# A fused LoRA feed-forward kernel: normalising the down projection's rows straight from PSUM

## The chip, the cores and the metric

One core of a Trainium2 chip runs the whole program. The metric is the device time of one execution in microseconds (us), taken as the median of several runs. The engines are named as in the profile: PE is TensorE's matrix multiply and PEld its weight load, DVE is VectorE, ACT is ScalarE, POOL is GpSimd, SP is the engine that issues most of the transfers.

## The reference

There are 4096 tokens: 128 entries of 32 tokens, 512 features each. Every entry has one of 16 LoRA adapters (rank 16, scale 0.5).

```python
def lora_add(base, inp, A, B):
    t = einsum('bri,bni->bnr', A[idx], inp)
    return base + einsum('bor,bnr->bno', B[idx], t) * 0.5
gate = lora_add(x @ W_gate.T, x, A_gate, B_gate)      # 512 -> 1376
up   = lora_add(x @ W_up.T,   x, A_up,   B_up)
act  = silu(gate) * up
down = lora_add(act @ W_down.T, act, A_down, B_down)  # 1376 -> 512
amax = clip(max(abs(down), axis=-1), 1e-5)            # per token
out  = ((down / amax) @ Wq.T) * (amax * weight_scale) + bias
result = x + out
```

`Wq` holds the four levels -1.5, -0.5, 0.5, 1.5.

## The kernel before, in words

The tokens, sorted by adapter, are worked through in 16 tiles of 256, each of two sub-tiles of 128 rows (`SUBS`, index `s`). The 1376 hidden features are cut into 11 chunks (`FC`, index `f`), the first 96 wide, the others 128. Every operand of a product is split into a high and a low part, and three matrix products (`PASSES`) stand for one.

Each engine has an instruction order of its own, written by hand, and semaphores tie the orders together. Tile 0 is coded apart, since it also brings in the weights; tiles 1 to 15 run in a loop. On the data of this profile no tile has more than two adapters, and the branch with `pair` true runs.

The feed-forward stage of a tile is not done at its end but inside the next tile's first chunks. In tile `t` PE does, in this order: chunk 0 of gate and up (`first_chunk_main`); the last chunk of the down projection of tile t-1 (`last_down`); chunk 1 of gate and a third of chunk 1 of up; the two LoRA products of chunk 0 (L1142); `lora_b_down(t-1)` (L1218), which completes `ps_down` for tile t-1 and counts up `blocks_done`; the rest of up 1 and the two LoRA products of chunk 1 (L1145); gate 2 with its LoRA product (L1145), up 2; the LoRA product of act chunk 0 (`lora_a_down`, L1189); and `down(t, 0)` (L1207), the first to write `ps_down` again. `ps_down` has one buffer, two PSUM banks, so `down(t, 0)` has to wait until the old contents have been taken out. After `down(t, 1)` PE transposes the normalised rows (`transpose_block`, L1229), and in later chunks multiplies them with `wq` (`ffn_block`).

Before, ACT copies both sub-tiles of `ps_down` to `norm` in SBUF (`drain_down`, L635, semaphore `drained`), and `down(t, 0)` waits for these two copies. `norm` is a part of the tensor `rows`, and the profile shows it under that name. DVE then finds each row's largest magnitude in `norm` (`block_scales`: a reduction over 512 columns at L854, a clip at L857, a reciprocal at L860 that counts up `rinv_ready`, a product at L861), and ACT scales `norm` in place (`normalise`, L639, semaphore `norm_ready`).

In the chunk loop ACT's order is `silu_gate(f)` (L696; L688 for chunk 0), `split_hi_b(f+2)` (L628), then the copies when f is 0, `split_hi_act(f)` (L707), then `normalise` when f is 1 or 2. DVE's order is `gate_times_up(f)` (L943; for chunk 0 `add_first_lora`, which ends with L937 and counts up `act_done`), `split_lo_b(f+2)` (L829), `split_lo_act(f)` (L949), `split_ad(f+1)` (L843, L845), then `block_scales(f)` when f is 0 or 1. POOL's `split_bd` (L561, L566) splits the LoRA rows of down as soon as `blocks_done` allows it. The last tile has no next one: there `block_scales` and `normalise` read `ps_down` already, and the diff leaves that part alone.

Of the kernel before, what the change touches and what calls it, by code (L numbers as in the profile page):

```python
# [35 lines left out]
ACT = mybir.ActivationFunctionType  # L36
# [50 lines left out]
def build(nc, x_tok, x_feat, lora_index, places, pair_masks, w_gu, w_down, w_2bit, a_gu, a_down, b_rows,  # L87
          scale_col, bias_rows,
          block_mask_in, identity_in, out):
    with ExitStack() as ctx:  # L90
# [138 lines left out]
        act_hi = sem("act_hi")  # L229
        act_lo = sem("act_lo")  # L230
        amax_steps = sem("amax_steps")
        drained = sem("drained")
        rinv_ready = sem("rinv_ready")
        norm_ready = sem("norm_ready")
        dt_hi = sem("dt_hi")
# [372 lines left out]
        def _(act):  # L608
# [20 lines left out]
                                     b_raw[0:n, at:at + 2 * w].rearrange("p (g w) -> p g w", g=2), ACT.Copy  # L629
                                     ).then_inc(b_hi, 1)  # L630

            def drain_down(tile, s):

                act.wait_ge(blocks_done, SUBS * tile + s + 1)
                nc.scalar.activation(norm[:, s, :], ps_down[:, s, :], ACT.Copy).then_inc(drained, 1)  # L635

            def normalise(tile, s, source):
                act.wait_ge(rinv_ready, SUBS * tile + s + 1)
                nc.scalar.activation(norm[:, s, :], source[:, s, :], ACT.Copy, scale=rinv[:, s:s + 1]  # L639
# [70 lines left out]
            def run_tile(tile, first, pair):  # L710

                if first:
                    if pair:
                        act.wait_ge(first_a_in, 32)
                    else:
                        act.wait_ge(a_in, a_loads(0, pair))
                    for k in range(KC):
                        nc.scalar.activation(a_split_chunk(0, k, loras(pair)), a_raw_chunk(k, loras(pair)),
                                             ACT.Copy).then_inc(a_hi, 1)
                act.wait_ge(x_in, 16 * ENTRIES * (tile + 1))  # L720
                if not first:
                    act.wait_ge(up_done, FC * tile)
                nc.scalar.activation(xs_split(0), x_by_chunk, ACT.Copy).then_inc(x_hi, 1)
                if first:
                    load_wgu(act, 2)
                    load_wd(act, 0)
                    load_wd(act, 1)
                    split_hi_wgu(2)
                    split_hi_t(tile, pair)
                    split_hi_b(tile, 0, pair)  # L730
                    split_hi_b(tile, 1, pair)
                    if pair:
                        copy_first_gate(tile, first)
                        copy_first_up(tile, first)
                    split_hi_wd(0)
                else:
                    split_hi_act(tile - 1, FC - 1, False)
                    split_hi_b(tile, 0, pair)
                    split_hi_b(tile, 1, pair)
                    if pair:  # L740
                        copy_first_gate(tile, first)
                        copy_down_lora(tile - 1)
                    split_hi_t(tile, pair)
                    if pair:
                        split_hi_down_lora(tile - 1)
                        copy_first_up(tile, first)
                for f in range(FC):
                    if first and 1 < f < FC - 1:
                        split_hi_wd(f + 1)
                    if first and 1 < f < FC - 2:  # L750
                        split_hi_wgu(f + 2)
                    silu_gate(tile, f, first, pair)
                    if first and f == 1:
                        split_hi_wgu(3)
                    if f < FC - 2:
                        split_hi_b(tile, f + 2, pair)
                    if not first and f == 0:
                        for s in range(SUBS):
                            drain_down(tile - 1, s)
                    if f < FC - 1:  # L760
                        split_hi_act(tile, f, first)
                    if first and f <= 1:
                        split_hi_wd(f + 1)
                    if not first and f in (1, 2):
                        normalise(tile - 1, f - 1, norm)
                    if not first and f in (2, 4):
                        split_hi_transposed(tile - 1, f // 2 - 1, ps_misc[:, :])

# [35 lines left out]
        def _(dve):  # L804
# [42 lines left out]
            def block_scales(tile, s, source):  # L847

                done = 2 * (SUBS * tile + s)
                if source is ps_down:  # L850
                    dve.wait_ge(blocks_done, SUBS * tile + s + 1)
                else:
                    dve.wait_ge(drained, SUBS * tile + s + 1)
                nc.vector.tensor_reduce(amax[:, s:s + 1], source[:, s, :], AX_X, ALU.max,  # L854
                                        apply_absolute_value=True).then_inc(amax_steps, 1)
                dve.wait_ge(amax_steps, done + 1)
                nc.vector.tensor_scalar(amax[:, s:s + 1], amax[:, s:s + 1], EPS, None, ALU.max  # L857
                                        ).then_inc(amax_steps, 1)
                dve.wait_ge(amax_steps, done + 2)
                nc.vector.reciprocal(rinv[:, s:s + 1], amax[:, s:s + 1]).then_inc(rinv_ready, 1)  # L860
                nc.vector.tensor_tensor(ascale[:, s:s + 1], amax[:, s:s + 1], wscale[:, :], ALU.mult  # L861
                                        ).then_inc(ffn_scaled, 1)
# [89 lines left out]
            def run_tile(tile, first, pair):  # L952

                if first:
                    for k in range(KC):
                        dve.wait_ge(a_hi, k + 1)
                        last = nc.vector.tensor_tensor(a_split_chunk(1, k, loras(pair)),
                                                       a_raw_chunk(k, loras(pair)),
                                                       a_split_chunk(0, k, loras(pair)).bitcast(F32), ALU.subtract)
                    last.then_inc(a_ready, 1)  # L960
                dve.wait_ge(x_hi, tile + 1)
                nc.vector.tensor_tensor(xs_split(1), x_by_chunk, xs_split(0).bitcast(F32), ALU.subtract
                                        ).then_inc(x_lo, 1)
                if first:
                    if not pair:
                        dve.wait_ge(mask_ready, 2)
                    mask_t(tile, pair)
                    split_lo_t(tile, pair)
                    split_lo_b(tile, 0, pair)
                    split_lo_wgu(2)  # L970
                    split_lo_b(tile, 1, pair)
                    split_lo_wd(0)
                else:
                    split_lo_act(tile - 1, FC - 1)
                    split_lo_b(tile, 0, pair)
                    split_lo_b(tile, 1, pair)
                    mask_t(tile, pair)
                    mask_down_lora(tile - 1, pair)
                    split_lo_t(tile, pair)
                    split_lo_down_lora(tile - 1, pair)  # L980
                split_ad(tile, 0, pair)
                for f in range(FC):
                    if first and 1 < f < FC - 1:
                        split_lo_wd(f + 1)
                        if f + 1 >= WQ_FROM:
                            convert_wq(f + 1 - WQ_FROM)
                    if first and 1 < f < FC - 2:
                        split_lo_wgu(f + 2)
                    if pair and f == 0:
                        add_first_lora(tile)  # L990
                    else:
                        gate_times_up(tile, f)
                    if first and f == 1:
                        split_lo_wgu(3)
                    if f < FC - 2:
                        split_lo_b(tile, f + 2, pair)
                    if f < FC - 1:
                        split_lo_act(tile, f)
                        split_ad(tile, f + 1, pair)
                    if first and f <= 1:  # L1000
                        split_lo_wd(f + 1)
                    if not first and f in (0, 1):
                        block_scales(tile - 1, f, norm)
                    if not first and f in (2, 4):
                        split_lo_transposed(tile - 1, f // 2 - 1, ps_misc[:, :])
                    if not first and f in (3, 5):
                        scale_and_bias(tile - 1, f // 2 - 1, ps_misc[:, :])
                if first:

                    dve.wait_ge(const_in, 48 if pair else 32)  # L1010
# [77 lines left out]
        def _(pe):  # L1088
# [110 lines left out]
            def down(tile, f, first):  # L1199
                w = WIDTHS[f]  # L1200
                if first:
                    pe.wait_ge(wd_lo, f + 1)
                elif f == 0:
                    pe.wait_ge(drained, SUBS * tile)
                for s in range(SUBS):
                    for n, (ap, wp) in enumerate(PASSES):
                        last = nc.tensor.matmul(ps_down[:, s, :], act_split[0:w, ap, f % 2, s * P:(s + 1) * P],  # L1207
# [162 lines left out]
```

## Time and profile before

| | |
|---|---|
| median of 3 runs | 966.0 us (965.61 to 966.6) |
| span of the profiled execution | 963.2 us |
| PE busy | 926.2 us, 96% of the span |
| DVE busy | 473.5 us, 49% |
| ACT busy | 337.6 us, 35% |
| POOL busy | 117.3 us, 12% |
| granted TensorE clock, mean | 0.994 |

The span runs from the first to the last instruction of the profiled execution. What lies around it, as far as the runs tell, is the difference to their median, 2.8 us. Times in the rows are us from the start of the span, durations are us unless the view says ns, and an instruction's start can lie a little ahead of the end of the one before it on the same engine, because engines are pipelined.

### The profile page before, as it was taken

What the parts mean: (1) busy time and instruction counts of PE and PEld (TensorE: products, weight loads), DVE (VectorE), ACT (ScalarE), POOL (GpSimd) and SP (SyncE); (2) the same over time, 40 slices, a digit from 0 to 9 for tenths busy, and PEclk for the clock granted to TensorE, in tenths of its full rate; (3) what the DMA queues carried; (4) which work ended last, traced back from release to release, by engine and by line L of the source; (5) the groups of instructions that cost most, each with busy time, mean ns of one, the idle gap of its engine ahead of it and who ended that gap; (6) DMA issues with size and microseconds to landing.
All of it is one profiled execution on the core that took longest, in us unless ns stands there. A gap on an engine that the chain in (4) does not pass through costs nothing.

```text
span 963.2 us, 21495 instructions
## 1 busy us (share of the span) xinstructions
PE 926.2 (96%) x6426; PEld 860.0 (89%) x6426; DVE 473.5 (49%) x1268; ACT 337.6 (35%) x778; POOL 117.3 (12%) x188
## 2 busy tenths in 40 slices
PE   4799999999999999999999999999999999999994
PEld 4799998999999999999999999999999999999993
DVE  3776345363543636345363643536354363634533
ACT  2545233242423425243242423325243242423421
POOL 0110200111010110200111020110200111020100
PEclk9999999999999999999999999999999999999998
DMA  4672212121121112212111121212212111221010
GB/s 135 196 203 58 63 40 58 36 54 44 47 61 37 53 34 58 58 42 58 36 53 43 50 61 37 58 26 61 55 44 58 36 52 42 52 61 36 23 33 25
DMA packets 56679, 54.83 MB, mean 57 GB/s; under 512 B 20080, under 2 KB 41968, under 8 KB 56656
## 3 DMA queue, kind: packets, MB, share of 16 engines
q1 hardware_dynamic: 55056, 52.08, 20.7%
q10 hardware_dynamic: 1600, 2.49, 0.8%
q8 instruction: 8, 0.13, 0.1%
q14 instruction: 15, 0.12, 0.0%
HBM read 46.14 MB, written 8.39 MB: 57 GB/s over the span
## 4 chain that ended last, share of the span: by engine, by line
PE 86%; DVE 5%; issue 3%; DMA 2%; SPq 2%; ACT 1%; DVEq 0%; ACTq 0%
PE ps_down L1207 24%; PE ps_up L1110 23%; PE ps_gate L1110 22%; PE ps_misc L1238 6%; PE ps_td L1189 4%; DVE b_split L829 2%; PE ps_gate L1145 2%; PE ps_up L1145 2%; PE ps_misc L1229 1%; DMA rows<-w_2bit 1%; DVE act_full L932 1%; ACT act_full L688 1%; DVE wgu L807 1%; DMA ad_raw<-pair_masks 1%; DMA rows<-w_down 0%
## 5 line engine op out<-in xcount | busy, mean ns | idle before, releaser
L1207 PE MATMUL ps_down<-wd,act_split 128*128 128x512 f32 (+1 forms) x1056 | 272.9, 394 | 0.0
L1110 PE MATMUL ps_up<-xs,wgu 128*128 128x256 f32 x1920 | 259.7, 284 | 0.0
L1110 PE MATMUL ps_gate<-xs,wgu 128*128 128x256 f32 x1920 | 258.4, 285 | 0.0
L1110 PEld LDWEIGHTS ps_gate<-xs,wgu 128*128 128x128 f32 x1920 | 248.8, 191 | 9.1
L1110 PEld LDWEIGHTS ps_up<-xs,wgu 128*128 128x128 f32 x1920 | 244.7, 192 | 1.3
L943 DVE TENSOR_TENSOR act_full<-ps_up,act_full 128x256 f32<-128x256 f32 x160 | 67.7, 423 | 309.7 <-PE ps_up L1145 309.7
L1207 PEld LDWEIGHTS ps_down<-wd,act_split 128*128 128x128 f32 (+1 forms) x1056 | 185.9, 188 | 31.1
L696 ACT ACTIVATE act_full<-ps_gate 128x256 f32<-128x256 f32 x160 | 60.5, 378 | 283.4 <-PE ps_gate L1145 283.4
L628 ACT ACTIVATE b_split<-b_raw 64x256 fp32r<-64x256 f32 (+1 forms) x176 | 70.2, 407 | 115.2 <-PE ps_up L1145 115.2
L707 ACT ACTIVATE act_split<-act_full 128x256 fp32r<-128x256 f32 (+1 forms) x176 | 73.1, 415 | 88.9 <-DVE act_full L943 84.1
L829 DVE TENSOR_TENSOR b_split<-b_raw,b_split 32x256 fp32r<-32x256 f32 (+1 forms) x176 | 86.9, 500 | 5.3 <-ACT b_split L628 0.4
L575 POOL TENSOR_TENSOR rows<-rows 128x512 f32<-128x512 f32 x30 | 38.7, 1289 | 358.0 <-DVE rows L924 358.0
L949 DVE TENSOR_TENSOR act_split<-act_full,act_split 128x256 fp32r<-128x256 f32 (+1 forms) x176 | 74.9, 425 | 13.2 <-ACT act_split L707 8.2
L1189 PE MATMUL ps_td<-act_split,ad_split 128*32 128x256 f32 (+1 forms) x352 | 69.5, 279 | 3.1 <-DVE act_split L949 3.1
L561 POOL TENSOR_TENSOR bd_split<-bd_raw,ones 64x512 fp32r<-64x512 f32 x16 | 16.9, 1057 | 430.2 <-PE ps_down L1218 388.9
L1238 PE MATMUL ps_misc<-wq,dt_split 128*128 128x512 f32 x248 | 62.7, 396 | 0.6 <-DVE dt_split L866 0.6
L1238 PEld LDWEIGHTS ps_misc<-wq,dt_split 128*128 128x128 f32 x248 | 47.6, 192 | 10.9 <-issue 0.9
L1145 PE MATMUL ps_gate<-t_split,b_split 96*128 96x256 f32 x160 | 47.2, 295 | 5.1 <-DVE b_split L829 5.1
L924 DVE SCALAR_TENSOR_TENSOR rows<-ps_misc,ascale,bias 128x512 f32<-128x512 f32 x31 | 23.3, 751 | 56.6 <-PE ps_misc L1238 56.6
L1189 PEld LDWEIGHTS ps_td<-act_split,ad_split 128*32 128x32 f32 (+1 forms) x352 | 43.0, 124 | 6.1 <-issue 4.3
L1145 PE MATMUL ps_up<-t_split,b_split 96*128 96x256 f32 x160 | 45.2, 282 | 0.0
L1145 PEld LDWEIGHTS ps_gate<-t_split,b_split 96*128 96x128 f32 x160 | 30.8, 192 | 8.2 <-DVE b_split L829 8.1
(90 smaller groups left out, 684.1 us busy)
## 6 DMA issues: line engine op xcount, KB each, us to landing
rows<-x_tok SPq DMA_DIRECT2D x128, 64.0 KB, 1.7
x_raw<-x_feat SPq DMA_DIRECT2D x124, 64.0 KB, 1.7
out<-rows SPq DMA_DIRECT2D x124, 64.0 KB, 1.6
b_raw<-b_rows SPq DMA_DIRECT2D x64, 92.0 KB, 2.9
b_raw<-b_rows SPq DMA_DIRECT2D x64, 80.0 KB, 2.5
rows<-w_gu SPq DMA_DIRECT2D x8, 512.0 KB, 4.1
rows<-w_down SPq DMA_DIRECT2D x9, 256.0 KB, 4.2
bd_raw<-b_rows SPq DMA_DIRECT2D x64, 32.0 KB, 1.7
```

The costliest lines, as they stand in the source:

```text
L575: pool.tensor_tensor(out_rows[:, s, :], x_res[:, s, :], out_rows[:, s, :], ALU.add).then_inc(out_ready, 1)
L628: nc.scalar.activation(b_split[0:n, 0, f % 2, :, 0:w], b_raw[0:n, at:at + 2 * w].rearrange("p (g w) -> p g w", g=2), ACT.Copy).then_inc(b_ ...
L696: nc.scalar.activation(act_full[0:w, f % 2, :], ps_gate[0:w, f % 2, 0:TILE], ACT.Silu).then_inc(silu_done, 1)
L707: nc.scalar.activation(act_split[0:w, 0, f % 2, :], act_full[0:w, f % 2, :], ACT.Copy).then_inc(act_hi, 1)
L829: nc.vector.tensor_tensor(lo, b_raw[0:n, at:at + 2 * w].rearrange("p (g w) -> p g w", g=2), b_split[0:n, 0, f % 2, :, 0:w].bitcast(F32), A ...
L943: nc.vector.tensor_tensor(act_full[0:w, f % 2, :], ps_up[0:w, f % 2, 0:TILE], act_full[0:w, f % 2, :], ALU.mult).then_inc(act_done, 1)
L949: nc.vector.tensor_tensor(act_split[0:w, 1, f % 2, :], act_full[0:w, f % 2, :], act_split[0:w, 0, f % 2, :].bitcast(F32), ALU.subtract).th ...
L1110: last = nc.tensor.matmul(ps_out[0:m, f % 2, 0:TILE], w, xs[:, xp, k, :], start=(start and k == 0), stop=(stop and k == KC - 1))
L1145: last = nc.tensor.matmul(ps_out[0:w, f % 2, 0:TILE], b_split[0:STACK, 0, f % 2, g, 0:w], t_split[0:STACK, 0, g, :], start=False, stop=True)
L1189: last = nc.tensor.matmul(ps_td[0:m, 0:TILE], ad_split[0:w, f % 2, 0:m], act_split[0:w, part, f % 2, :], start=(f == 0 and part == HI), st ...
L1207: last = nc.tensor.matmul(ps_down[:, s, :], act_split[0:w, ap, f % 2, s * P:(s + 1) * P], wd[0:w, wp, f, :], start=(f == 0 and n == 0), st ...
L1238: last = nc.tensor.matmul(ps_block, dt[:, part, k, :], wq[:, k, :], start=(part == HI and k == 0), stop=(part == LO and k == KC - 1))
```

## The change

The two copies of `ps_down` go. `block_scales` and `normalise` of tile t-1 read `ps_down` itself, as they did already in the last tile. `block_scales(0)` and `block_scales(1)` move up on DVE, to just behind the product of gate and up of chunks 0 and 1. `normalise(0)` and `normalise(1)` move up on ACT by one chunk, to the end of chunks 0 and 1. The next tile's first write to `ps_down` waits for `norm_ready`, for both sub-tiles, in place of `drained`.

```diff
-            def drain_down(tile, s):
-
-                act.wait_ge(blocks_done, SUBS * tile + s + 1)
-                nc.scalar.activation(norm[:, s, :], ps_down[:, s, :], ACT.Copy).then_inc(drained, 1)
...
-                    if not first and f == 0:
-                        for s in range(SUBS):
-                            drain_down(tile - 1, s)
                     if f < FC - 1:
                         split_hi_act(tile, f, first)
                     if first and f <= 1:
                         split_hi_wd(f + 1)
-                    if not first and f in (1, 2):
-                        normalise(tile - 1, f - 1, norm)
+                    if not first and f in (0, 1):
+                        normalise(tile - 1, f, ps_down)
...
             def block_scales(tile, s, source):
-                if source is ps_down:
-                    dve.wait_ge(blocks_done, SUBS * tile + s + 1)
-                else:
-                    dve.wait_ge(drained, SUBS * tile + s + 1)
+                dve.wait_ge(blocks_done, SUBS * tile + s + 1)
...
                         gate_times_up(tile, f)
                     if first and f == 1:
                         split_lo_wgu(3)
+                    if not first and f in (0, 1):
+                        block_scales(tile - 1, f, ps_down)
                     if f < FC - 2:
                         split_lo_b(tile, f + 2, pair)
...
-                    if not first and f in (0, 1):
-                        block_scales(tile - 1, f, norm)
...
                 elif f == 0:
-                    pe.wait_ge(drained, SUBS * tile)
+                    pe.wait_ge(norm_ready, SUBS * tile)
```

## Rows read from the trace of the kernel before

**Rows 1.** Busy time by engine over one steady tile: us, busy (instructions), clock, DMA

```profile
200.00:257.58 57.58, 57.23 (x402) 53.32 (x401) 27.90 (x77) 20.04 (x47) 7.46 (x12) 1.00 0.19 48
```

**Rows 2.** Waits of PE from 84 to 940 us: total us, times, longest

```profile
PE ps_gate L1145 <- DVE b_split L829: 5.1, 15, 0.3
```

**Rows 3.** Timeline around one change of tile: start, duration, engine, line

```profile
257.83 1.03 POOL L561 TENSOR_TENSOR bd_split<-bd_raw,ones 64x512 fp32r<-64x512 f32 x1 [26.17 <-PE ps_down L1218]
...
258.20 0.94 DVE L937 TENSOR_TENSOR act_full<-ad_raw,act_full 96x256 f32<-96x256 f32 x1 [0.16 <-ACT act_full L688]
...
258.38 1.05 ACT L635 ACTIVATE rows<-ps_down 128x512 f32<-128x512 f32 x2
...
258.94 1.36 POOL L566 TENSOR_TENSOR bd_split<-bd_raw,bd_split 32x512 fp32r<-32x512 f32 x1
259.17 1.41 DVE L829 TENSOR_TENSOR b_split<-b_raw,b_split 32x256 fp32r<-32x256 f32 x1
...
259.64 0.37 ACT L696 ACTIVATE act_full<-ps_gate 128x256 f32<-128x256 f32 x1
...
260.61 0.42 DVE L949 TENSOR_TENSOR act_split<-act_full,act_split 96x256 fp32r<-96x256 f32 x1
...
260.63 0.39 PE L1145 MATMUL ps_gate<-t_split,b_split 96*128 96x256 f32 x1 [0.34 <-DVE b_split L829]
...
261.27 0.68 DVE L854 TENSOR_REDUCE amax<-rows 128x1 f32<-128x512 f32 x1
...
262.31 0.42 DVE L943 TENSOR_TENSOR act_full<-ps_up,act_full 128x256 f32<-128x256 f32 x1
262.40 1.25 PEld L1207 LDWEIGHTS ps_down<-wd,act_split 96*128 96x128 f32 x6
...
262.76 0.42 DVE L829 TENSOR_TENSOR b_split<-b_raw,b_split 32x256 fp32r<-32x256 f32 x1
...
263.08 0.71 ACT L639 ACTIVATE rows<-rows,rinv 128x512 f32<-128x512 f32 x1
...
263.70 0.36 ACT L696 ACTIVATE act_full<-ps_gate 128x256 f32<-128x256 f32 x1
...
263.92 0.26 PEld L1189 LDWEIGHTS ps_td<-act_split,ad_split 128*32 128x32 f32 x2
```

**Rows 4.** Timeline of the last tile's end, where the source is PSUM already

```profile
945.65 0.69 DVE L854 TENSOR_REDUCE amax<-ps_down 128x1 f32<-128x512 f32 x1
...
946.56 0.16 DVE L860 RECIPROCAL rinv<-amax 128x1 f32<-128x1 f32 x1
...
946.76 0.69 ACT L639 ACTIVATE rows<-ps_down,rinv 128x512 f32<-128x512 f32 x1 [0.36 <-DVE rinv L860]
...
947.50 0.42 PEld L1229 LDWEIGHTS ps_gate<-ad_raw,rows 128*128 128x128 f32 x4 [0.63 <-ACT rows L639]
```

**Rows 5.** Timeline of POOL and DVE in tile 0

```profile
43.70 2.16 POOL L566 TENSOR_TENSOR bd_split<-bd_raw,bd_split 32x512 fp32r<-32x512 f32 x1
...
44.63 0.41 DVE L943 TENSOR_TENSOR act_full<-ps_up,act_full 128x256 f32<-128x256 f32 x1
45.07 1.07 DVE L829 TENSOR_TENSOR b_split<-b_raw,b_split 32x256 fp32r<-32x256 f32 x1
```

**Rows 6.** One DVE line: ns shortest/median/longest, first and last start

```profile
L820 DVE TENSOR_SCALAR wq<-rows x4: 427/427/540, 58.0 to 73.0; 128x512 fp32r<-128x512 int32 x4
```

**Rows 7.** Timeline of PE in tile 0, its two longest waits there

```profile
26.46 0.46 PE L1142 MATMUL ps_misc<-t_split,b_split 96*96 96x256 f32 x2 [3.02 <-DVE b_split L829]
...
41.27 0.39 PE L1189 MATMUL ps_td<-act_split,ad_split 128*32 128x256 f32 x2 [1.48 <-DVE act_split L949]
```

**Rows 8.** Windows of tile 0: columns as in rows 1

```profile
24.00:28.00 4.00, 1.54 (x8) 1.57 (x9) 2.89 (x5) 2.98 (x7) 0.00 (x0) 0.85 0.40 123
28.00:32.00 4.00, 4.00 (x26) 3.92 (x26) 3.65 (x12) 2.28 (x6) 0.00 (x0) 0.73 0.35 111
...
41.40:45.00 3.60, 3.60 (x26) 3.34 (x26) 2.74 (x4) 2.13 (x4) 2.73 (x2) 1.00 0.74 244
```

More of the change, by code:

```diff
@@ L231, in build @@
         amax_steps = sem("amax_steps")
-        drained = sem("drained")
         rinv_ready = sem("rinv_ready")
```

## The prediction, made before the changed kernel was run

> **What bounds the kernel now.** I read three views in this order. The windows come first, with a window as long as one steady tile: PE is busy 57.23 of 57.58 us at the full clock of 2.4 GHz (granted share 1.00), and DVE and ACT are busy for half of that or less [rows 1]. The reader is to see that a steady tile has 0.35 us in which PE does nothing. The table of waits names it: from tile 1 to near the end PE waits for one thing only, DVE's split of the LoRA rows of chunk 2, 15 times 0.34 us [rows 2, 3]. So PE's order sets the time, and an edit can gain at most 5.1 us in the steady tiles, while every wait that it adds to PE costs its full length, 15 times over (the wait in the diff stands in tiles 1 to 15). The timeline around one change of tile is then the working sheet. I follow the tile whose `blocks_done` lets POOL go at 257.83; the other 14 tiles of the loop show the same pattern.
>
> In that sheet the reader is to see who holds whom. POOL runs L561 until 258.86 and L566 until 260.30. DVE's L937 begins at 258.20 and ends at 259.14, which is 0.28 us behind the first of these ends; DVE's L829 takes 1.41 us in place of 0.42 and ends at 260.58, 0.28 us behind the second [rows 3]. DVE operations with two inputs in SBUF stand still while POOL works, and run after it.
>
> **What the change removes.** Two ACT copies, 1.05 us for both (L635, 258.38 to 259.43) [rows 3]. ACT is no bound, and PE waited for none of its results in the steady tiles [rows 2], so nothing is gained by that. The old wait on `drained` had ended at 259.43, while PE came to `down(t, 0)` at 262.40 (first weight load of L1207) [rows 3]: 3 us of cover, and no gain from its removal either.
>
> **What the change adds.** PE now needs both normalised sub-tiles at 262.40. I lay out the new order link by link, with durations for PSUM sources from the last tile's end, where the same instructions already read `ps_down` [rows 4]. There the reduction starts at 945.65 and the reciprocal ends at 946.72: 1.07 us from start to `rinv_ready`. ACT starts 0.04 us later, takes 0.69 us (ends 947.45), and PE starts 0.05 us after that. From SBUF the reduction takes 0.68 and the scaling 0.71 [rows 3], so the source as such changes next to nothing.
>
> 1. DVE ends L937 at 259.14 and turns to the first reduction at 259.17 (where L829 started before). Its reciprocal ends at 259.17 + 1.07 = 260.24.
> 2. ACT is through with the high part of act 0 by then (0.41 us from 259.17) and starts `normalise(0)` at 260.28. The SiLU of chunk 1 stands behind it in ACT's order. Behind a `normalise` the next SiLU starts 0.62 us after it (263.08 to 263.70) and takes 0.37 us [rows 3]: 260.90 to 261.27. Before, this SiLU ended at 260.01.
> 3. DVE, meanwhile: `block_scales` occupies 1.04 us (261.27 to 262.31) [rows 3], so L829 comes up at 260.21, is held to 260.30 as before and ends at 260.58 to 260.65. The delayed reduction thus falls into time in which L829 stood still anyway, and the old PE wait of 0.34 us stays about as it is. L949 and the split of A follow, 0.66 us as before (260.61 to 261.27) [rows 3]. DVE is free at 261.28 to 261.35.
> 4. Both roads meet: `gate_times_up(1)` (L943) starts at 261.30, one us before the 262.31 of before. The next DVE instruction starts 0.45 us behind it (262.31 to 262.76) [rows 3]: the second reduction at 261.75, its reciprocal done at 262.82.
> 5. ACT starts `normalise(1)` at 262.86 (the high part of act 1, released at 261.72, is long done), ends at 263.55, and PE starts `down(t, 0)` at 263.60.
>
> Against 262.40 that is **1.20 us of new waiting per tile**. Fifteen tiles give 18.0 us. The terms that I am sure of to a few hundredths are the two reductions and the two scalings; pipelining at the joints gives or takes 0.1 us, so 1.1 to 1.3 us per tile and 16.5 to 19.5 us.
>
> What is late next? The low part of act 1 now ends at 261.75 + 1.04 + 0.45 + 0.43 = 263.67. It is wanted by `lora_a_down(1)`, which came 1.52 us behind the first load of L1207 (263.92) [rows 3], now at 265.12: covered by 1.4 us. The transposes wanted `norm_ready` after that and find it. The diff adds no transfers and moves none, and past the wait PE's order is as before, so nothing comes back: PE had 0.34 us of waiting per tile, and that lies ahead of the new wait.
>
> **The row that I lack.** In step 1 the clip L857 (a `tensor_scalar` on one column) would come up at 259.88, while POOL still works until 260.30. No row shows that instruction under a busy POOL. From below: it runs freely, as a DVE product with one input in PSUM does (L943 at 44.63 takes its usual 0.41 us inside L566) [rows 5]. From above: it is held to 260.30, as the two-input L829 was at 45.07 (1.07 us) [rows 5], and as a `tensor_scalar` over 512 columns seems to be, with 540 ns at its longest against 427 [rows 6]. Held, it ends at 260.35, the reciprocal at 260.55, ACT's `normalise(0)` starts at 260.59, the SiLU ends at 261.58 and L943 starts at 261.64: 0.34 us later, 1.54 us per tile, 23.1 us in all. I take the free value, since one column gives little to share, and keep the other for the range.
>
> The Trainium skill (SBUF — State Buffer, section "Who interferes with whom") says that VectorE and GpSimd share a pair of SBUF ports under an exclusive lock, and that a `tensor_scalar`, unlike a reduction, can enter a mode that takes the pair. The trace agrees for L829, with 1.41 against 0.42 us; for one column no run here shows it. By that rule the sum would be 23.1 us, by the free value 18.0 us.
>
> **The rivals.**
>
> *A, the forecast:* the wait for the rows is 1.2 us per tile. Chance 0.57.
>
> *B, the clip is held by POOL:* 1.54 us per tile, 966.0 + 23.1 = 989.1 us. For it: the 540 ns of L820 [rows 6]. Against it: a one-column instruction. Chance 0.22. This is also where the skill's rule for `tensor_scalar` would put it.
>
> *C, the first reduction is held by POOL as a whole:* it then runs from 260.30 rather than 259.17, its last 0.53 us or more after POOL's end. Up to 1.13 us later at step 1, 2.2 to 2.3 us per tile, about 34 us: 1000 us. Against it: its input lies in PSUM, and L943, whose one input does too, wasn't held [rows 5]. Chance 0.05.
>
> *D, the clock falls behind each new wait.* In tile 0 a PE wait of 3.02 us [rows 7] is followed by granted shares of 0.85 and 0.73 in two windows of 4 us [rows 8]; that is (0.15 + 0.27) x 4 = 1.7 us lost, an estimate, at the lower level of 1.2 GHz for a part of them. Fifteen times that on top of A is 25 us: 1009 us. Against it: behind the wait of 1.48 us that ended at 41.27 the share was 1.00 [rows 7, 8], and mine is shorter. Chance 0.04.
>
> *E, not slower: the rows are ready in time.* Reading PSUM would have to shorten the three links that read `ps_down` on the path (both reductions, the second scaling; 0.69 us each, 2.07 together) by 1.2 us, each to about 0.29 us. Then the cost is nothing and the time 966 us; only beyond that point could the lighter ACT show at all, and at most the 5.1 us of rows 2 would be in reach. Against it: the last tile's rows at 0.69 us [rows 4]. Chance 0.04, of which 0.02 for a gain.
>
> The remaining 0.08 is for a wait shorter or longer than any of these by a joint that I misread, such as a SiLU that isn't late.
>
> **How the numbers follow.** My 963.2 us span is 2.8 us below the median of the runs; the added time lies inside the span, so it goes on the median: 966.0 + 18.0 = **984.0 us**, a span of 981.2 us. A alone has 982.5 to 985.5 us. The range reaches up to B and a little past it, and down by 0.2 us per tile for the joints: 980.5 to 990.5 us, which leaves out C, D, E and half of the remainder. 0.2% (2 us) is about what a measurement of this kernel can tell from no change. Slower: 0.96 (A to D and the remainder). Same 0.02, faster 0.02 (E).
>
> **What would show it.** PE's table of waits gets a new row, `down` (L1207) held by ACT's L639, 15 times some 1.2 us, or 1.5 if B holds; the wait on L829 stays near 0.3. The SiLU of chunk 1 follows `normalise(0)` on ACT. L857 of the first sub-tile takes 0.15 us in A, about 0.5 in B. The reduction takes 0.69 us, far more in C. The clock stays at 1.00, except in D. L635 is gone. The prediction is wrong if PE shows no wait at L1207, or if a later wait in the tile has shrunk by as much.

## The result and the profile after

The changed kernel takes 983.7 us (median of 4 runs, 983.08 to 984.71) beside 965.95 us for the kernel before (4 runs): a ratio of 1.0183, 95% interval 1.017 to 1.0195. The forecast was 984.0 us. The span of the profiled execution grew from 963.2 to 981.7 us.

First, one steady tile. The columns of the window are those of [rows 1]; the two rows from PE's timeline are the first LoRA products of chunk 0 in tile 2 and in tile 15, 13 tiles apart.

```profile
200.23:259.00 58.77, 57.48 (x402) 53.29 (x402) 27.10 (x77) 19.48 (x46) 7.46 (x12) 1.00 0.17 47
```

```profile
143.18 0.40 PE L1130 MATMUL ps_misc<-t_split,b_split 96*96 96x256 f32 x2
...
907.15 0.40 PE L1130 MATMUL ps_misc<-t_split,b_split 96*96 96x256 f32 x2
```

The reader is to see (907.15 - 143.18) / 13 = 58.77 us per tile in place of 57.58 [rows 1], at the same 402 instructions of PE and at a clock of 1.00: 1.19 us more, and 15 x 1.19 = 17.9 us. The medians differ by 983.7 - 965.95 = 17.75 us. ACT lost its copies (20.04 to 19.48 us busy per tile), and that bought nothing.

The table of PE's waits, from 84 to 958 us, has the row that was forecast, and it has a second that has grown (5.1 us in [rows 2]):

```profile
PE ps_down L1195 <- ACT rows L633: 11.5, 15, 0.8
PE ps_gate L1133 <- DVE b_split L820: 7.8, 15, 0.5
```

The timeline around one change of tile, the counterpart of [rows 3]. POOL's first split starts at 261.76, where it started at 257.83 there, so subtracting 3.93 puts these times beside the sheet of the prediction.

```profile
261.76 1.03 POOL L560 TENSOR_TENSOR bd_split<-bd_raw,ones 64x512 fp32r<-64x512 f32 x1 [26.16 <-PE ps_down L1206]
...
262.14 0.94 DVE L925 TENSOR_TENSOR act_full<-ad_raw,act_full 96x256 f32<-96x256 f32 x1 [0.15 <-ACT act_full L682]
...
262.87 1.36 POOL L565 TENSOR_TENSOR bd_split<-bd_raw,bd_split 32x512 fp32r<-32x512 f32 x1
263.00 0.67 DVE L842 TENSOR_REDUCE amax<-ps_down 128x1 f32<-128x512 f32 x1
...
263.71 0.15 DVE L845 TENSOR_SCALAR amax<-amax 128x1 f32<-128x1 f32 x1
263.90 0.16 DVE L848 RECIPROCAL rinv<-amax 128x1 f32<-128x1 f32 x1
263.98 0.27 DVE L849 TENSOR_TENSOR ascale<-amax,wscale 128x1 f32<-128x1 f32 x1
264.10 0.69 ACT L633 ACTIVATE rows<-ps_down,rinv 128x512 f32<-128x512 f32 x1 [0.57 <-DVE rinv L848]
264.28 0.42 DVE L820 TENSOR_TENSOR b_split<-b_raw,b_split 32x256 fp32r<-32x256 f32 x1
264.68 0.38 ACT L690 ACTIVATE act_full<-ps_gate 128x256 f32<-128x256 f32 x1
...
264.75 0.38 PE L1133 MATMUL ps_gate<-t_split,b_split 96*128 96x256 f32 x1 [0.53 <-DVE b_split L820]
...
265.39 0.42 DVE L931 TENSOR_TENSOR act_full<-ps_up,act_full 128x256 f32<-128x256 f32 x1
265.72 0.68 DVE L842 TENSOR_REDUCE amax<-ps_down 128x1 f32<-128x512 f32 x1
...
266.28 0.23 PEld L1177 LDWEIGHTS ps_td<-act_split,ad_split 96*64 96x64 f32 x2
...
266.82 0.69 ACT L633 ACTIVATE rows<-ps_down,rinv 128x512 f32<-128x512 f32 x1 [0.56 <-DVE rinv L848]
...
267.56 1.22 PEld L1195 LDWEIGHTS ps_down<-wd,act_split 96*128 96x128 f32 x6 [1.05 <-ACT rows L633]
```

Three things are to be seen. PE's first weight load for the next down product stands 0.05 us behind the end of the second scaling (266.82 + 0.69 = 267.51): the rows set that moment. That scaling follows the second reduction, which follows the product of gate and up of chunk 1 at 265.39, which follows all that DVE does after the first reduction at 263.00. And the clip L845 takes its 0.15 us although POOL works from 262.87 to 264.23.

### The profile page after: what moved, and what is told of

Same layout as the page of the kernel before. It is cut to its first block, busy times and chain, and to the rows that moved or that the text cites. A ratio compares the mean times of both kernels' runs of the same rounds, so it can differ in the third digit from the quotient of the medians.

```text
span 981.7 us, 21465 instructions
## 1 busy us (share of the span) xinstructions
PE 932.1 (95%) x6426; PEld 862.0 (88%) x6426; DVE 461.5 (47%) x1268; ACT 329.1 (34%) x748; POOL 117.1 (12%) x188
## 4 chain that ended last, share of the span: by engine, by line
PE 82%; DVE 7%; issue 3%; ACT 2%; SPq 2%; DMA 2%; DVEq 0%; ACTq 0%
PE ps_down L1195 24%; PE ps_gate L1098 22%; PE ps_up L1098 21%; PE ps_misc L1226 6%; PE ps_td L1177 4%; DVE amax L842 2%; PE ps_up L1133 2%; PE ps_gate L1133 2%; PE ps_misc L1217 1%; ACT rows L633 1%; DMA rows<-w_down 1%; DVE b_split L820 1%; DVE act_split L937 1%; DVE act_full L920 1%; ACT act_full L682 1%
## 5 line engine op out<-in xcount | busy, mean ns | idle before, releaser
L1195 PE MATMUL ps_down<-wd,act_split 128*128 128x512 f32 (+1 forms) x1056 | 274.2, 395 | 11.5 <-ACT rows L633 11.5
L1195 PEld LDWEIGHTS ps_down<-wd,act_split 128*128 128x128 f32 (+1 forms) x1056 | 185.5, 188 | 46.6 <-ACT rows L633 15.7
L820 DVE TENSOR_TENSOR b_split<-b_raw,b_split 32x256 fp32r<-32x256 f32 (+1 forms) x176 | 72.2, 416 | 5.3 <-ACT b_split L627 0.4
L1177 PE MATMUL ps_td<-act_split,ad_split 128*32 128x256 f32 (+1 forms) x352 | 69.4, 278 | 3.3 <-DVE act_split L937 3.3
L1177 PEld LDWEIGHTS ps_td<-act_split,ad_split 128*32 128x32 f32 (+1 forms) x352 | 43.0, 124 | 5.9 <-issue 4.2
```

Of the source, the lines that this page charges most:

```text
L820: nc.vector.tensor_tensor(lo, b_raw[0:n, at:at + 2 * w].rearrange("p (g w) -> p g w", g=2), b_split[0:n, 0, f % 2, :, 0:w].bitcast(F32), A ...
L1177: last = nc.tensor.matmul(ps_td[0:m, 0:TILE], ad_split[0:w, f % 2, 0:m], act_split[0:w, part, f % 2, :], start=(f == 0 and part == HI), st ...
```

## The experiments

Three theories stand against each other in the expectations. **W**: the price is PE's wait for the normalised rows, which come out of the end of a chain through the in-order queues of DVE and ACT. **M**: the price is that block_scales and normalise were moved ahead of other work, whatever PE waits for. **S**: the price is the reading of PSUM. The times beside each are medians, with the ratio to the kernel before on the same chip.

### The moves alone, with the old wait

The kernel before, with its copies and its wait on `drained`; the scales and the scaling stand where the change puts them.

```diff
+                    if not first and f in (0, 1):
+                        block_scales(tile - 1, f, norm)
                     if f < FC - 2:
                         split_lo_b(tile, f + 2, pair)
...
-                    if not first and f in (0, 1):
-                        block_scales(tile - 1, f, norm)
...
-                    if not first and f in (1, 2):
-                        normalise(tile - 1, f - 1, norm)
+                    if not first and f in (0, 1):
+                        normalise(tile - 1, f, norm)
```

> The kernel before, with its two copies and its old wait for them, but block_scales and normalise moved to the places that the change gives them (reading the copies in SBUF). Theory W (the new wait on the normalised rows is the price): PE's wait at the first down product is gone, what stays is the later split of the LoRA rows (0.53 in place of 0.34 us of waiting per tile, so 15 x 0.19 = 2.9 us): 968.9 us. Rival M (moving the scales ahead on DVE and ACT is the price, whatever PE waits for): near the changed kernel, 982 to 985 us. Rival S (reading PSUM is the price): 966 us, since nothing but the copies reads PSUM here.

Measured: 968.57 us, ratio 1.0026 (1.0015 to 1.0037). In its timeline the second scaling is as late as in the change, and PE has passed by then:

```profile
263.72 1.25 PEld L1207 LDWEIGHTS ps_down<-wd,act_split 96*128 96x128 f32 x6
...
264.02 0.72 ACT L639 ACTIVATE rows<-rows,rinv 128x512 f32<-128x512 f32 x1 [0.56 <-DVE rinv L860]
```

The scaling ends at 264.74, and PE begins `down` at 263.72 without a wait. So the moves cost about 2.8 us (968.57 against 965.74 in these runs), and the other 15 of the 17.75 us need the wait on the normalised rows. M is out as the main cause.

### Waiting for each sub-tile by itself

```diff
-                elif f == 0:
-                    pe.wait_ge(norm_ready, SUBS * tile)
                 for s in range(SUBS):
+                    if not first and f == 0:
+                        pe.wait_ge(norm_ready, SUBS * (tile - 1) + s + 1)
```

> The changed kernel, but the next tile's down product waits for each sub-tile by itself: three products on the first bank behind the first normalised sub-tile, three on the second behind the second. Theory W: the first sub-tile is ready long before (its scaling ends at 264.79, PE comes near 266.5), and three products of 0.215 us lie ahead of the second wait, so 0.65 us of the wait is hidden. Left: 1.2 - 0.65 = 0.55 us per tile, 8.3 us: 974.2 us. Rivals M and S: no change from 983.7 us.

Measured: 973.15 us, ratio 1.0078 (1.006 to 1.0096). The six weight loads of `down` fall apart into two groups of three:

```profile
263.55 0.55 PEld L1195 LDWEIGHTS ps_down<-wd,act_split 96*128 96x128 f32 x3
...
263.86 0.69 ACT L633 ACTIVATE rows<-ps_down,rinv 128x512 f32<-128x512 f32 x1 [0.57 <-DVE rinv L848]
...
264.59 0.53 PEld L1195 LDWEIGHTS ps_down<-wd,act_split 96*128 96x128 f32 x3 [0.50 <-ACT rows L633]
```

The chain through DVE and ACT is the same, sources and moves too. Three products were put in the place of idle time, and 10.5 us came back. It is the second sub-tile alone that PE waits for.

### Both scales early

The second block_scales no longer stands behind the product of gate and up of chunk 1, nor the second scaling behind the high part of act 1.

```diff
-                    if not first and f in (0, 1):
-                        block_scales(tile - 1, f, ps_down)
+                    if not first and f == 0:
+                        block_scales(tile - 1, 0, ps_down)
                     if f < FC - 2:
                         split_lo_b(tile, f + 2, pair)
+                    if not first and f == 0:
+                        block_scales(tile - 1, 1, ps_down)
...
+                    if not first and f == 1:
+                        normalise(tile - 1, 1, ps_down)
                     if f < FC - 1:
                         split_hi_act(tile, f, first)
...
-                    if not first and f in (0, 1):
-                        normalise(tile - 1, f, ps_down)
+                    if not first and f == 0:
+                        normalise(tile - 1, 0, ps_down)
```

> The changed kernel, but the second block_scales comes right behind the split of the LoRA rows of chunk 2, ahead of the split of act 0, and the second normalise ahead of the high part of act 1: neither waits for gate times up of chunk 1 any more. Theory W: in the time of the sheet the second reduction starts at 260.80, the rows are ready at 262.65 against 262.59 when PE comes, so only the 0.19 us of the later LoRA split and some 0.06 us of the rows remain: 0.25 us per tile, 969.7 us. Rival M: the scales sit even earlier, so at least as slow as the change, 984 us or more. Rival S: 983.7 us.

Measured: 968.74 us, ratio 1.0032 (1.0021 to 1.0044). The wait on `norm_ready` still stands in the code, and the rows are still read from PSUM, but PE's table has no row for it any more; the one that is left is the LoRA split:

```profile
262.92 0.39 PE L1137 MATMUL ps_gate<-t_split,b_split 96*128 96x256 f32 x1 [0.52 <-DVE b_split L822]
...
264.01 0.69 ACT L633 ACTIVATE rows<-ps_down,rinv 128x512 f32<-128x512 f32 x1 [0.48 <-DVE rinv L850]
...
264.75 1.23 PEld L1199 LDWEIGHTS ps_down<-wd,act_split 96*128 96x128 f32 x6
```

The load of `down` comes 0.05 us behind the end of the scaling (264.70), and 0.27 us behind the load ahead of it at 264.48, where it is 0.23 in the kernel before: PE and the rows now arrive almost together. So 15 of the 17.75 us are the place of the second half in the two queues. This run moves it in both at once; in the change ACT sat idle for 0.56 us before its second scaling, so there it was DVE's queue that set the moment.

### The SiLU ahead of the first scaling

```diff
                     silu_gate(tile, f, first, pair)
+                    if not first and f == 1:
+                        normalise(tile - 1, 0, ps_down)
...
-                    if not first and f in (0, 1):
-                        normalise(tile - 1, f, ps_down)
+                    if not first and f == 1:
+                        normalise(tile - 1, 1, ps_down)
```

> The changed kernel, but ACT does the SiLU of chunk 1 ahead of the first normalise. The sheet had two roads to gate times up of chunk 1: the SiLU behind the first normalise, and DVE's own queue (split of the LoRA rows, of act 0 and of A), both ending at 261.3. The trace of the change has the SiLU done at 265.06 and DVE free at 265.39, so DVE's queue is the later one: no change, 983.7 us within 1 us. Rival (the SiLU behind the scaling is what delays the second half): 0.4 us or more per tile come back, 978 us or less.

Measured: 983.67 us, ratio 1.0192 (1.0175 to 1.0209), as the change. The SiLU is done early now, and the product of gate and up is not:

```profile
263.40 0.36 ACT L690 ACTIVATE act_full<-ps_gate 128x256 f32<-128x256 f32 x1
...
265.24 0.19 DVE L838 TENSOR_TENSOR ad_split<-ad_raw,ad_split 128x32 fp32r<-128x32 f32 x1
265.35 0.42 DVE L933 TENSOR_TENSOR act_full<-ps_up,act_full 128x256 f32<-128x256 f32 x1
```

Of the two roads of step 4, DVE's own queue is the later one; ACT's order is free here.

### POOL's split held back, in the change

```diff
                     pool.wait_ge(blocks_done, SUBS * tile)
+                    pool.wait_ge(down_done, FC * tile + 2)
```

> The changed kernel, but POOL's split of the down LoRA rows also waits until the second down product of the tile is through, so that it no longer runs beside this chain on DVE. Theory W with POOL's hold as a part of it: DVE's last product of chunk 0 ends 0.52 us sooner, PE loses its wait on the LoRA split (0.5 us), and the rows are ready 0.5 us sooner: the wait on the rows is then 1.07 us from a PE that is 0.34 us ahead of the kernel before, 0.73 us net per tile, 977 us. If POOL's hold has no part in it: 983.7 us.

Measured: 973.68 us, ratio 1.0082 (1.0061 to 1.0104), 3.3 us less than worked out. The direction is right: with POOL out of the way DVE's last product of chunk 0 takes 0.42 us (0.94 in the change), and the wait on the LoRA split is gone from PE's table. What stays there is the wait on the rows:

```profile
259.05 0.42 DVE L926 TENSOR_TENSOR act_full<-ad_raw,act_full 96x256 f32<-96x256 f32 x1 [0.15 <-ACT act_full L683]
...
263.83 1.23 PEld L1196 LDWEIGHTS ps_down<-wd,act_split 96*128 96x128 f32 x6 [1.04 <-ACT rows L634]
```

The idle time before PE's weight load is 1.04 us, about what it is in the change (1.05). Both ends moved by about as much: the rows come sooner, and PE does too. PE's weight loads show that the LoRA split is still a little late:

```profile
259.42 1.51 PEld L1099 LDWEIGHTS ps_gate<-xs,wgu 128*128 128x128 f32 x12
...
261.02 0.19 PEld L1134 LDWEIGHTS ps_gate<-t_split,b_split 96*128 96x128 f32 x1
```

The load for the LoRA product comes 1.60 us behind the first of the twelve ahead of it. The next run, in which it isn't held, has 1.44 us there, so 0.16 us of this wait are left, and the table doesn't show them.

### POOL's split held back, in the kernel before

The same line in the kernel before.

> The kernel before, with POOL's split of the down LoRA rows held back until the second down product of the tile. Theory W, whose sheet has POOL hold DVE's two-input operations: DVE's split of the LoRA rows of chunk 2 ends at about 259.1 in place of 260.58, PE's wait of 0.34 us there is gone, 15 times: 961 us. If POOL isn't what holds DVE: 966 us.

Measured: 957.22 us, ratio 0.9918 (0.9904 to 0.9931). PE has no wait left in the steady tiles, and tiles 2 and 15 stand here:

```profile
141.42 0.40 PE L1143 MATMUL ps_misc<-t_split,b_split 96*96 96x256 f32 x2
...
882.22 0.40 PE L1143 MATMUL ps_misc<-t_split,b_split 96*96 96x256 f32 x2
```

(882.22 - 141.42) / 13 = 56.98 us per tile, 0.60 less than before, where the table of waits named 0.34 [rows 2, 3]. The expectation of 961 us came from that 0.34, and so did the 977 us of the run above. The weight loads show the whole of it; first the kernel before, then this run:

```profile
258.57 1.51 PEld L1110 LDWEIGHTS ps_gate<-xs,wgu 128*128 128x128 f32 x12
...
260.63 0.19 PEld L1145 LDWEIGHTS ps_gate<-t_split,b_split 96*128 96x128 f32 x1 [0.55 <-DVE b_split L829]
```

```profile
257.17 1.51 PEld L1111 LDWEIGHTS ps_gate<-xs,wgu 128*128 128x128 f32 x12
...
258.61 0.19 PEld L1146 LDWEIGHTS ps_gate<-t_split,b_split 96*128 96x128 f32 x1
```

From the first of the twelve loads to the load of the LoRA product it is 2.06 us before and 1.44 us here, 0.62 us less. Run once more beside the last experiment:

> The kernel before with POOL's split held back, once more beside the run without waits, on the same chip: 957 us, and by theory W equal to that run.

Measured: 956.07 us, ratio 0.9895 (0.9879 to 0.9911), with the same tile length.

### Both together, and the change without any wait

Early scales and POOL's split held back:

> The change with the second block_scales and normalise early (as in the run with the scales together) and POOL's split held back. Theory W: the LoRA split is in time (260.11 against 260.29), the rows are ready at 261.99 against PE at 262.06, so no wait is left at either place and the time is that of the kernel before with POOL held back, 961 us. If reading PSUM or the missing copies cost anything by themselves, it is above that run by as much.

Measured: 958.86 us, ratio 0.9932 (0.9919 to 0.9945), 1.6 us above the kernel before with POOL's split held back (957.22), with intervals that overlap. PE's table has no wait left, but the weight loads show two joints that are late:

```profile
257.84 1.51 PEld L1103 LDWEIGHTS ps_gate<-xs,wgu 128*128 128x128 f32 x12
...
259.44 0.19 PEld L1138 LDWEIGHTS ps_gate<-t_split,b_split 96*128 96x128 f32 x1
...
261.00 0.21 PEld L1182 LDWEIGHTS ps_td<-act_split,ad_split 96*64 96x64 f32 x2
...
261.27 1.21 PEld L1200 LDWEIGHTS ps_down<-wd,act_split 96*128 96x128 f32 x6
```

The load for the LoRA product comes 1.60 us behind the first of the twelve rather than 1.44, and `down` 0.27 us behind the load before it rather than 0.23 (262.17 to 262.40 in the kernel before). So the expectation that no wait is left was wrong by some 0.2 us per tile, of which 0.15 us stay in the length of the tile (57.13 against 56.98 us). The 961 us was too high for the reason given above.

Then the change with everything that the runs had named:

```diff
+                    pool.wait_ge(down_done, FC * tile + 2)
...
+                    if not first and f == 1:
+                        for s in range(SUBS):
+                            normalise(tile - 1, s, ps_down)
                     if f < FC - 1:
                         split_hi_act(tile, f, first)
...
                     if f < FC - 2:
                         split_lo_b(tile, f + 2, pair)
+                    if not first and f == 0:
+                        for s in range(SUBS):
+                            block_scales(tile - 1, s, ps_down)
...
                 for s in range(SUBS):
+                    if not first and f == 0:
+                        pe.wait_ge(norm_ready, SUBS * (tile - 1) + s + 1)
```

(The old places of block_scales, normalise and the wait are taken out.)

> The change freed of all its waits: POOL's split held back, both block_scales behind the split of the LoRA rows of chunk 2, both normalise between the LoRA rows of chunk 3 and the high part of act 1, and the down product waiting per sub-tile. Theory W: PE finds everything ready, the steady tile is as long as in the kernel before with POOL held back (56.99 us), and so is the time, 957.2 us within 1 us. Rival S (reading PSUM by DVE and ACT, or the copies' absence, has a price of its own): above that by the price.

Measured: 958.43 us, ratio 0.9922 (0.9907 to 0.9936). Its tiles:

```profile
141.64 0.40 PE L1133 MATMUL ps_misc<-t_split,b_split 96*96 96x256 f32 x2
...
883.51 0.40 PE L1133 MATMUL ps_misc<-t_split,b_split 96*96 96x256 f32 x2
```

(883.51 - 141.64) / 13 = 57.07 us, 0.09 more than the kernel before with POOL held back. Its timeline has one late joint: the low part of act 0 stands behind both scales on DVE and ends at 260.59, and PE's next load follows it.

```profile
259.11 1.51 PEld L1101 LDWEIGHTS ps_up<-xs,wgu 128*128 128x128 f32 x12
...
260.18 0.41 DVE L939 TENSOR_TENSOR act_split<-act_full,act_split 96x256 fp32r<-96x256 f32 x1
...
260.70 0.16 PEld L1180 LDWEIGHTS ps_td<-act_split,ad_split 96*64 96x64 f32 x2
```

The twelve loads before it start 0.12 us apart from 259.11, the last at 260.43, so the next was due at 260.55 and came at 260.70. A part of the 0.15 us is made up at once: `down` is loaded at 260.88, 0.18 us behind, where 0.23 is usual. What remains, 0.10 us, accounts for the 0.09 us. So a price of reading PSUM, if there is one, is within 0.09 us per tile or 1.3 us in all, and S can't account for 17.75 us. The medians put this run 1.2 us above the first and 2.4 us above the second run of the kernel before with POOL held back, with intervals that overlap. The change gains nothing even without its waits: ACT, which it relieves, was waited for by no one.

## Why the prediction was right, point by point

**What bounds the kernel** was read rightly in kind: PE sets the time, and an added wait costs its length 15 times over. One number of that part failed: "an edit can gain at most 5.1 us in the steady tiles". Holding back POOL alone gained 0.60 us per tile, 9 us in the steady tiles. The 0.34 us is the time from the modelled end of the last product before to the start of the next one. That end lies 0.28 us behind its start, while the products follow one another at 0.12 us when nothing holds them: 0.16 us of the wait don't show. And where nothing holds it, a weight load starts 0.12 us ahead of its product (258.61 and 258.73 with POOL's split held back); here both start at 260.63. Together that is 0.34 + 0.16 + 0.12 = 0.62 us, as the loads have it. What a wait costs is the start that came against the start that was due, best read from the weight loads.

**What it removes** (nothing gained): right. PE waits for no copy in any run, and the run with the copies and the moves is 2.8 us slower than the kernel before, with no copy on the path.

**What it adds**, link by link, all on the clock of the sheet (the measured start less 3.93):

| link | forecast | measured |
|---|---|---|
| first reduction starts | 259.17 | 259.07 |
| first reciprocal ends | 260.24 | 260.13 |
| LoRA split of chunk 2 ends | 260.58 to 260.65 | 260.77 |
| SiLU of chunk 1 ends | 261.27 | 261.13 |
| gate times up of chunk 1 starts | 261.30 | 261.46 |
| second reduction starts | 261.75 | 261.79 |
| second scaling starts | 262.86 | 262.89 |
| PE's first load of `down` | 263.60 | 263.63 |

The end is right to 0.03 us, but by joints that are off both ways, and that they cancel so closely is luck. The first reduction started 0.10 us sooner than the sheet. DVE's queue is then 0.16 us later than the sheet at gate times up: the product L849 took 0.27 us, held by POOL, where it takes 0.14 at its quickest, and the split of the LoRA rows came up behind it. That also raised PE's wait there from 0.34 to 0.53 us, where I wrote that it stays about as it is; by the moves-only run this part is 0.19 us of the 1.19. It adds nothing to the total, since the rows and not PE set the moment at which `down` starts. In return the second reduction followed 0.33 us behind the product, not 0.45. The two roads do not meet: DVE's is 0.33 us later than ACT's (265.39 against 265.06), which the run with the SiLU first bears out.

**The missing row** is there now. L845 under a busy POOL took 0.15 us, so B is out. The Trainium skill (SBUF — State Buffer, section "Who interferes with whom") says that a `tensor_scalar` can take the shared ports and that a DVE instruction with two SBUF inputs contends with a GpSimd instruction that reads SBUF. The trace agrees with the second part even for one column (L849, 0.27 against 0.14 us); a one-column `tensor_scalar` was not held here, and the measurement decides.

**The rivals.** C is out (the reduction took 0.67 us inside L565). D is out (granted share 1.00 in the steady tile with the new wait). E is out (0.67 to 0.69 us for each link that reads PSUM). The range's lower end, 980.5 us, is 0.5 us below what 0.2 us per tile give (981.0 us); nothing rests on that.

**What would show it.** The row L1195 behind ACT's scaling is there 15 times, but with 0.77 us rather than 1.2. The missing part is no gain: 0.19 us went to the LoRA split ahead of it, and the rest is the same reading error as above, since idle time before a product starts from a modelled end. Going by weight loads, `down` was due 0.23 us behind L1177 (266.51, by the spacing of the kernel before) and came at 267.56: 1.05 us. In the kernel before that spacing lies between this load and the one at 262.40 [rows 3]:

```profile
262.17 0.23 PEld L1189 LDWEIGHTS ps_td<-act_split,ad_split 96*64 96x64 f32 x2
```


What stays open: the exact sharing of 1.19 us between the two waits is by the moves-only run and the loads, which agree to 0.05 us, and no finer; the 0.09 us per tile by which the change without waits is longer than the kernel before with POOL held back are put down to one joint by its trace, and that was not tried by a run.

## What to carry to other kernels

When a buffer is to be freed by a later step in place of a copy, list everything that stands ahead of that step on its in-order engines: here the second half of the rows stood behind a product that had nothing to do with it, and moving it ahead gave back 15 of 17.75 us. Relieving an engine for which nobody waits buys nothing, so put the single-buffered resource first. Look for a helper engine that runs early without need: holding POOL's split back by one line made the kernel before faster by 0.8 and 1.05% in its two runs, which have the lowest medians of all (957.22 and 956.07 us).

## What the runs showed of the hardware that was not expected

- The idle time before a matmul understates a wait: 0.34 us in the table, 0.60 us per tile when the wait was gone.
- POOL holds a DVE product of one column by two SBUF inputs (0.27 against 0.14 us) and lets a one-column clip (0.15 us) and a 512-column reduction pass, be the reduction's source in PSUM (0.67 us here) or in SBUF. The second is seen in the moves-only run, where POOL's split runs from 260.08 to 261.44:

```profile
260.08 1.36 POOL L566 TENSOR_TENSOR bd_split<-bd_raw,bd_split 32x512 fp32r<-32x512 f32 x1
260.21 0.67 DVE L854 TENSOR_REDUCE amax<-rows 128x1 f32<-128x512 f32 x1
```

- A reduction can start before the DVE instruction ahead of it has ended, 0.08 us here (263.00 against 262.14 + 0.94), and 0.33 us behind the start of a 0.42 us product.
